# Self-attention's copies before the last rows' high parts, table steps behind the context's row maxima, and the first chunk's weights before the row sums

## The chip, the cores and the metric

The kernel runs on one core of a Trainium2 chip. The metric is the device time of one execution in microseconds (us), lower is better. The same program was timed several times, and each kernel also ran once under the hardware profiler.

## The reference

One decoder layer in float32 on x (16 sequences of 112 rows, 1024 wide) and a context (16 x 375 rows, 1024 wide):

```python
qkv = x @ Wqkv + bqkv                       # q, k, v: 256 wide, one head
x = layernorm(x + softmax(q @ k.T / 16) @ v @ Wo + bo)
Q = x @ Wq.T + bq;  K = ctx @ Wk.T + bk
x = layernorm(x + softmax(Q @ K.T / 32) @ ctx)
Wg, Wu, Wd = dequant(4-bit words, scales, zeros, g_idx)   # FFN, 2752 wide
x = layernorm(x + (silu(x @ Wg) * (x @ Wu)) @ Wd)
```

Matrix products are made in float16 with every operand split into a high and a low part, in three passes (high x high, high x low, low x high).

## The kernel before

Five engine programs are written out by hand, each in its own order, and meet through semaphores. PE is the tensor engine, DVE the vector engine, ACT the scalar engine, POOL is GpSimd, and SP issues most DMAs.

**Self-attention** goes over four groups of four sequences (448 rows). Group 0 stands alone, groups 1 and 2 are one loop on PE, ACT and SP, and group 3 stands alone. In a group PE makes four products for q and k (called f = 0 to 3, 24 matmuls each, into two PSUM banks in turn), the v rows of sequence 0, the scores, the v rows of sequences 1 to 3 (`v_rows`, 24 matmuls each), transposes of the probabilities (L1690), the first half of the transposes of the next group's rows (L1640), the products of probabilities and v, the second half of those transposes, and the output product of each sequence. ACT copies each q/k product out of PSUM (L1371); product f may start when copy f - 2 is made. On DVE a group begins with the largest of the next group's rows (`x_max`, L497), which POOL takes over the partitions, and the low part of the last rows of the group before. Then come the scores' maxima (L543), four steps on the next group's factor (`x_factor`, L512 to L515, which wait for POOL), the reciprocal of the exponentials' sums (L550), the probabilities (L552), two copies of v out of PSUM (L556) and the copy of the transposed probabilities (L561). Then DVE splits the next group's rows (L490) and normalises the four sequences' sums one after the other.

Each normalised sequence is also stored in two float16 parts. ACT makes the high part (`x1_hi`, L1365), which needs the normalised rows and a buffer that an earlier store has to leave. `x1_hi` of sequences 0 to 2 stands at the end of a group's ACT program, and that of sequence 3 behind the copy of f = 0 of the next group.

**Table steps.** The FFN's scales, zeros and indices are made into tables once. `table_rows` runs on DVE in group 1, `table_parts` in group 2 and `select` in group 3, each ahead of the wait for the scores. They are 80-odd short DVE instructions, each waiting for the one before. SP stores their results and reads parts of them back.

**Preparation of cross-attention.** PE multiplies the two weight matrices in float32 (M, eight pieces of 32 matmuls, L1647), POOL takes sums over the same weights (L1213 to L1223), and ACT asks for the next piece of weights (L1415) once PE and POOL have read the last. DVE takes the largest of the first context's rows (L779 and L784), then waits for PE's row of maxima (L789), which stands behind the sixth piece.

**FFN.** 22 chunks of 128 hidden columns. Chunks 0 to 3 multiply gate and up for four groups of 448 rows (t = 0 to 3). The weights of chunk i + 1 (numbers q = 3i + 2 and 3i + 3) and the down weights of chunk i (number 3i + 4) are unpacked meanwhile: PE gathers scales and zeros (L1825, L1899), DVE masks the words (L830, L837) and scales them (L850, L852), ACT and POOL make the parts (L1456, L1245). A gather waits until the weights before it are scaled, because they share PSUM. In the same four chunks the rows' sums for later chunks are made for two sequences each: POOL `row_sums` (L1310 to L1315), ACT `sum_hi` (L1555), DVE `sum_lo` (L1022). `hidden` is silu on ACT, the product with up on DVE, and its parts (L864, L875).

## Time and profile before

| | |
|---|---|
| median of 3 runs | 1846.81 us (1845.61 to 1848.7) |
| the profiled execution: its time, its span | 1848.76 us, 1847.0 us |
| PE busy | 1737.1 us, 94% of the span |
| DVE, ACT, POOL busy | 1069.9 (58%), 494.4 (27%), 502.6 us (27%) |
| mean granted clock of PE | 0.99 of full speed |

The page gives busy time per engine, the span in 40 slices with the granted clock, and the chain of work that ended last. In time order the stages are self-attention (to about 239 us), preparation (to about 367), cross-attention (to about 701), the FFN's products (to about 1445) and the down product. In the last two PE hardly ever waits.

### The profile page before, as it was taken

The numbers are of one execution on the slowest core, as the hardware profiler recorded it, in microseconds if no ns is written. First come the engines' busy times: TensorE is split into PE (matmuls) and PEld (weight loads), VectorE is DVE, ScalarE is ACT, GpSimd is POOL, SyncE is SP. The second block draws the span as 40 slices with busy tenths as digits, with TensorE's granted clock in tenths as the row PEclk, the third lists the DMA queues.
The fourth block names the chain that finished last, engine by engine and source line by source line (L and its number), as shares of the span: only waits on it lengthen the run. The fifth ranks groups of instructions, "written<-read, shape, count | busy, mean of one in ns | idle before, by whom it ended". The sixth has DMA issues, their size and how long they took to land.

```text
span 1847.0 us, 26676 instructions
## 1 busy us (share of the span) xinstructions
PE 1737.1 (94%) x9784; PEld 979.2 (53%) x9784; DVE 1069.9 (58%) x1656; ACT 494.4 (27%) x734; POOL 502.6 (27%) x326
## 2 busy tenths in 40 slices
PE   5898899897899988998999999999999899999998
PEld 3666644486777754444444444444445344444443
DVE  7788550656788875667777777787775211111111
ACT  3222210354555543233323323233232100000000
POOL 0221378223333425543323223223231000000000
PEclk9999999999999999999999999999999999999999
DMA  9342571599999977763231321322313822122120
GB/s 324 102 130 80 158 205 34 120 209 231 225 236 239 232 166 156 179 143 80 56 88 48 81 62 48 95 48 62 81 45 79 324 101 107 53 106 106 53 106 23
DMA packets 335590, 231.89 MB, mean 126 GB/s; under 512 B 288224, under 2 KB 302624, under 8 KB 333348
## 3 DMA queue, kind: packets, MB, share of 16 engines
q1 hardware_dynamic: 329284, 227.85, 47.8%
q10 hardware_dynamic: 6240, 3.15, 0.6%
q8 instruction: 43, 0.70, 0.2%
q14 instruction: 23, 0.19, 0.0%
HBM read 122.93 MB, written 60.83 MB: 99 GB/s over the span
## 4 chain that ended last, share of the span: by engine, by line
PE 45%; issue 28%; DVE 11%; SPq 6%; DMA 5%; POOL 3%; ACT 1%; DVEq 0%; POOLq 0%; ACTq 0%
PE psum L1647 44%; SPq L2178 4%; DMA arena<-arena 3%; DMA arena<-in_x 2%; DVE arena L810 1%; POOL small L1162 1%; POOL arena L1171 1%; PE psum L1899 1%; PE psum L1825 1%; DVE arena L1016 1%; DVE arena L1014 1%; DVE arena L1011 1%; DVE arena L875 1%; DMA x_parts_scratch<-arena 1%; SPq L2085 1%
## 5 line engine op out<-in xcount | busy, mean ns | idle before, releaser
L1647 PE MATMUL psum<-arena 128*128 128x448 f16 (+6 forms) x7176 | 1273.0, 338 | 50.7 <-DMA arena<-arena 24.6
L1647 PEld LDWEIGHTS psum<-arena 128*128 128x128 f16 (+3 forms) x7176 | 752.3, 109 | 552.8 <-issue 89.4
L2002 PE MATMUL psum<-arena 128*128 128x512 f16 x1820 | 393.5, 379 | 6.4 <-DMA arena<-down_weights_scratch 3.7
L2002 PEld LDWEIGHTS psum<-arena 128*128 128x128 f16 x1820 | 177.7, 98 | 222.2 <-DMA arena<-down_weights_scratch 5.4
L1245 POOL TENSOR_TENSOR arena<-arena 128x1024 f16<-128x1024 f32 (+1 forms) x60 | 149.8, 2509 | 417.0 <-ACT arena L1456 417.0
L1144 DVE SCALAR_TENSOR_TENSOR arena<-psum,small,arena 128x512 f32<-128x512 f32 x28 | 20.9, 751 | 331.9 <-PE psum L2002 331.9
L1162 POOL TENSOR_TENSOR small<-small 112x1 f32<-112x1 f32 (+1 forms) x46 | 50.9, 1107 | 510.7 <-DVE small L471 510.7
L1547 ACT ACTIVATE arena<-arena,small 128x448 f32<-128x448 f32 x68 | 45.5, 668 | 208.6 <-DVE arena L1076 145.2
L1456 ACT ACTIVATE arena<-arena 128x1024 f16<-128x1024 f32 (+1 forms) x60 | 68.8, 1173 | 120.2 <-DVE arena L852 91.9
L1236 POOL TENSOR_TENSOR arena<-arena 128x224 f16<-128x224 f32 x64 | 55.6, 869 | 124.9 <-ACT arena L1427 124.8
L850 DVE TENSOR_TENSOR arena<-arena,psum 128x1024 f32<-128x1024 uint32 x65 | 79.1, 1217 | 2.9 <-PE psum L1825 0.9
L852 DVE TENSOR_TENSOR arena<-arena,psum 128x1024 f32<-128x1024 f32 x65 | 79.3, 1221 | 2.2
L1475 ACT ACTIVATE arena<-arena 128x448 f16<-128x448 f32 (+1 forms) x88 | 50.7, 576 | 103.7 <-DVE arena L864 103.7
L875 DVE TENSOR_TENSOR arena<-arena 128x448 f16<-128x448 f32 (+1 forms) x88 | 56.8, 646 | 36.8 <-ACT arena L1475 36.8
L779 DVE TENSOR_REDUCE small<-arena 128x1 f32<-128x1024 f32 (+1 forms) x48 | 58.0, 1216 | 26.5 <-DMA arena<-in_ctx 26.1
L810 DVE SCALAR_TENSOR_TENSOR arena<-arena,small 128x1024 f16<-128x1024 f32 (+1 forms) x48 | 61.2, 1279 | 12.0 <-ACT arena L1433 12.0
L1433 ACT ACTIVATE arena<-arena,small 128x1024 f16<-128x1024 f32 (+1 forms) x48 | 51.8, 1138 | 46.3 <-DVE small L806 46.3
L466 DVE BATCH_NORM_STATS2 small<-arena 112x6 f32<-112x512 f32 (+1 forms) x92 | 58.8, 681 | 1.4 <-DVE small L806 1.1
L482 DVE TENSOR_SCALAR arena<-arena,small 112x1024 f32<-112x1024 f32 (+1 forms) x46 | 44.3, 964 | 25.1 <-POOL small L1162 25.1
L864 DVE SCALAR_TENSOR_TENSOR arena<-arena,small 128x448 f32<-128x448 f32 (+1 forms) x72 | 49.0, 680 | 13.4 <-ACT arena L1484 10.6
L830 DVE TENSOR_TENSOR arena<-arena,small 128x1024 uint32<-128x1024 uint32 x43 | 55.8, 1297 | 0.3
L1252 POOL TENSOR_TENSOR arena<-arena 128x1024 f16<-128x1024 f32 x21 | 44.8, 2132 | 40.0 <-ACT arena L1464 40.0
(213 smaller groups left out, 1207.3 us busy)
## 6 DMA issues: line engine op xcount, KB each, us to landing
h_scratch<-arena SPq DMA_DIRECT2D x84, 224.0 KB, 2.9
arena<-h_scratch SPq DMA_DIRECT2D x13, 1376.0 KB, 6.0
arena<-in_ctx SPq DMA_DIRECT2D x32, 512.0 KB, 5.2
arena<-in_x SPq DMA_DIRECT2D x32, 448.0 KB, 5.6
x_scratch<-arena SPq DMA_DIRECT2D x32, 448.0 KB, 3.6
arena<-x_scratch SPq DMA_DIRECT2D x32, 448.0 KB, 4.7
arena<-in_L_ffn_down_qweight SPq DMA_DIRECT2D x21, 512.0 KB
down_weights_scratch<-arena SPq DMA_DIRECT2D x20, 512.0 KB, 3.8
```

Of the source, the lines that this page charges most:

```text
L466: dve.bn_stats(st[0:n, 6 * h:6 * h + 6], y[:, h * HALF:(h + 1) * HALF]).then_inc(s_st, 1)
L779: ins = dve.tensor_reduce(cmx[0:CP[c], c:c + 1], cx[0:CP[c], c, :], AX.X, ALU.max, apply_absolute_value=True)
L810: dve.scalar_tensor_tensor(cxp[b % 2][0:CP[c], c, 1, :], cx[0:CP[c], c, :], fc[0:CP[c], b:b + 1], cxp[b % 2][0:CP[c], c, 0, :], ALU.mult, ...
L850: dve.tensor_tensor(w, w.bitcast(U32), zeros, ALU.subtract).then_inc(s_dq, 1)
L852: dve.tensor_tensor(w, w, scales, ALU.mult).then_inc(s_wf if done is None else done, 1)
L875: dve.tensor_tensor(h_st[0:n, 1, cols], h_f[0:n, :], h_st[0:n, 0, cols], ALU.subtract).then_inc(s_hl, 1)
L1162: pool.tensor_tensor(rstd[0:n, :], ve[0:n, :], mhalf[0:n, :], ALU.pow).then_inc(s_rstd, 1)
L1245: return pool.tensor_tensor(dst[:, :, 1, :], wf32[:, lo * HALF:hi * HALF].rearrange("p (c n) -> p c n", n=P), dst[:, :, 0, :], ALU.subtract)
L1456: return act.activation(wgu[s][:, lo * 4:hi * 4, 0, :], wf32[:, lo * HALF:hi * HALF].rearrange("p (c n) -> p c n", n=P), ACT.Identity)
L1647: mm = pe.matmul(out, a, r, start=(k == 0), stop=(k == len(pairs) - 1))
L2002: mm = pe.matmul(bk[2 * s + c], ht[s][:, i, a, :], weights_of(i, w, c), start=(i == 0 and (w, a) == PASSES[0]), stop=(i == NI - 1 and (w, ...
L2178: sp.dma_start_transpose(cxt[s].rearrange("p l k t -> p (l k) t")[:, :, c * P:(c + 1) * P], cxp[s][:, c, :, :].rearrange("p l d -> p (l d) ...
```

## The change

1. **Self-attention, ACT.** In the loop groups `x1_hi` of sequence 2 goes from the end of a group to behind the copy of f = 0 of the next group, and that of sequence 3 from behind f = 0 to behind f = 1.
2. **Self-attention, PE and DVE.** `v_rows(3)` goes behind the transposes of the probabilities. DVE does the first v copy, then `x_factor`, then the copy of the transposed probabilities, then the second v copy.
3. **Table steps.** The second part of `table_rows` (now `row_numbers`), `table_parts` and `select` leave groups 1, 2 and 3 and stand between the largest of the first context's rows and the wait for PE's row of maxima. SP's twelve stores of tables go behind the loads of the first context. One memset goes behind the steps, since its place overlaps what they read.
4. **Chunk 0.** DVE scales the up weights of chunk 1 before `hidden(0, 1)` and the first pair's sums, and scales the down weights before the second pair's sums. ACT does `hidden` before `sum_hi` to match.

```diff
@@ dve, self_attention
                 dve.tensor_scalar(nm1[0:S, :], mx1[0:S, :], HD ** -0.5, None, ALU.mult).then_inc(s_nm, 1)
-                if more:
-                    x_factor(g + 1)
                 dve.wait_ge(s_exp, GB * g + GB)
...
+                    if p == 0 and more:
+                        x_factor(g + 1)
+                    if p == 0:
+                        dve.wait_ge(s_pt, g + 1)
+                        dve.tensor_copy(pt[0:S, :, :], bk[4][0:S, 0:TG].rearrange("p (b k) -> p b k", b=GB)
+                                        ).then_inc(s_pte, 1)
...
-            self_attention(2, True, (table_parts,))
-            self_attention(NG - 1, False, (select,))
+            self_attention(2, True)
+            self_attention(NG - 1, False)
...
             for c in range(CC):
                 context_max(0, c)
+            row_numbers()
+            table_parts()
+            select()
+
+            dve.memset(cxp[1][96:P, CC - 1, :, :], 0.0)
             context_largest(0)
@@ dve, chunk
+                if known(i, 1):
+
+                    scaled(q + 1, 1)
+                    hidden(i, 1)
                 for p in pair(i, 0):
                     sum_lo(p)
...
                     masked(down_no(i), 2, s, i)
+                if known(i, 1):
+                    hidden(i, 2)
+                    scaled(down_no(i), 2)
                 for p in pair(i, 1):
                     sum_lo(p)
@@ act, self_attention
-                    if f == 0 and not known(g, 1):
-                        x1_hi(g * GB - 1, GB - 1, 2 * g)
+                    if f < 2 and not known(g, 1):
+                        x1_hi(g * GB - 2 + f, GB - 2 + f, 2 * g)
...
-                for b in range(GB - 1):
+                for b in range(GB - 2 if more else GB - 1):
                     x1_hi(g * GB + b, b, 2 * g + b // 2 + 1)
@@ pe, self_attention
-                for b in range(1, GB):
-                    mm = v_rows(b)
-                    if b % 2:
-                        mm.then_inc(s_v, 1)
+                v_rows(1).then_inc(s_v, 1)
+                v_rows(2)
...
                 mm.then_inc(s_pt, 1)
+                v_rows(3).then_inc(s_v, 1)
```

ACT, from the last `x1_hi` of the loop group to the copies of group 3 (group 3's side shows what stands there in a row). Before:

```order
L1365 ACTIVATE arena<-arena 112x1024
L1404 REGISTER_ALU
L1404 COMPARE_AND_BRANCH
L1371 ACTIVATE arena<-psum,small 128x448
L1365 ACTIVATE arena<-arena 112x1024
L1371 ACTIVATE arena<-psum,small 128x448 x3
```

And now (lines have moved in the changed kernel: L1389 is the copy, L1383 `x1_hi`):

```order
L1383 ACTIVATE arena<-arena 112x1024 x2
L1422 REGISTER_ALU
L1422 COMPARE_AND_BRANCH
L1389 ACTIVATE arena<-psum,small 128x448
L1383 ACTIVATE arena<-arena 112x1024
L1389 ACTIVATE arena<-psum,small 128x448
L1383 ACTIVATE arena<-arena 112x1024
L1389 ACTIVATE arena<-psum,small 128x448 x2
```

Two high parts now stand between the copies, each one copy later, and two instead of three at the group's end.

DVE in chunk 0, from the unpacking of chunk 1's gate weights to the sums of the second pair (L830 and L837 mask, L850 and L852 scale, L1022 is `sum_lo`, L864 and L875 are `hidden`). Before:

```order
L850 TENSOR_TENSOR arena<-arena,psum 128x4x2x128
L852 TENSOR_TENSOR arena<-arena,psum 128x4x2x128
L830 TENSOR_TENSOR arena<-arena,small 128x1024
L1022 SCALAR_TENSOR_TENSOR arena<-arena 112x1024 x2
L864 SCALAR_TENSOR_TENSOR arena<-psum,small,arena 128x448
L875 TENSOR_TENSOR arena<-arena 128x448
L850 TENSOR_TENSOR arena<-arena,psum 128x4x2x128
L852 TENSOR_TENSOR arena<-arena,psum 128x4x2x128
L837 TENSOR_SCALAR arena<-arena,small 128x1024
L1022 SCALAR_TENSOR_TENSOR arena<-arena 112x1024 x2
```

And now (L834, L841, L854, L856, L1030, L868 and L879 are the same lines):

```order
L834 TENSOR_TENSOR arena<-arena,small 128x1024
L854 TENSOR_TENSOR arena<-arena,psum 128x4x2x128
L856 TENSOR_TENSOR arena<-arena,psum 128x4x2x128
L868 SCALAR_TENSOR_TENSOR arena<-psum,small,arena 128x448
L879 TENSOR_TENSOR arena<-arena 128x448
L1030 SCALAR_TENSOR_TENSOR arena<-arena 112x1024 x2
L841 TENSOR_SCALAR arena<-arena,small 128x1024
L868 SCALAR_TENSOR_TENSOR arena<-psum,small,arena 128x448
L879 TENSOR_TENSOR arena<-arena 128x448
L854 TENSOR_TENSOR arena<-arena,psum 128x1024
L856 TENSOR_TENSOR arena<-arena,psum 128x1024
L1030 SCALAR_TENSOR_TENSOR arena<-arena 112x1024 x2
```

The up weights of chunk 1 are scaled two `sum_lo` and one `hidden` earlier.

DVE between the context's row maxima and PE's row of maxima. Before, L789 stood directly behind L784:

```order
L956 MEMSET small 128x4
L957 MEMSET small 128x1
L779 TENSOR_REDUCE small<-arena 128x1 x2
L779 TENSOR_REDUCE small<-arena 119x1
L784 TENSOR_REDUCE small<-small 128x1
L789 TENSOR_REDUCE small<-psum 128x1
```

Now 77 table steps begin behind L788 (the L784 of before); these are the last of them, the memset and what was L789:

```order
L676 MEMSET arena 128x256 x2
L677 MEMSET arena 128x512
L685 TENSOR_SCALAR arena<-arena,small 128x128 x4
L687 TENSOR_SCALAR arena<-arena,small 128x2752
L688 TENSOR_SCALAR arena<-arena,small 128x64
L967 MEMSET arena 32x1024
L793 TENSOR_REDUCE small<-psum 128x1
```

29 of the steps left group 1, 42 left group 2 and six left group 3.

## Rows read from the trace of the kernel before

**Rows 1.** Waits of PE over the whole span: us in total, times, longest.

```profile
PE psum L1647 <- DMA arena<-arena: 24.6, 14, 2.9
PE psum L1647 <- ACT arena L1371: 11.2, 5, 4.6
PE psum L1690 <- DVE arena L556: 5.1, 2, 3.0
PE psum L1647 <- DMA arena<-in_L_xattn_Wq: 0.8, 1, 0.8
```

**Rows 2.** Timeline of PE: start, length, engine, line, form, count, idle before and releaser.

```profile
39.98 21.30 PE L1647 MATMUL psum<-arena 128*128 128x448 f16 x160 [0.33 <-ACT arena L1371]
63.37 0.57 PE L1690 MATMUL psum<-ident,arena 112*112 112x112 f32 x4 [2.09 <-DVE arena L556]
...
93.90 22.76 PE L1647 MATMUL psum<-arena 128*128 128x448 f16 x160 [4.09 <-ACT arena L1371]
...
147.59 22.99 PE L1647 MATMUL psum<-arena 128*128 128x448 f16 x160 [4.64 <-ACT arena L1371]
173.57 0.60 PE L1690 MATMUL psum<-ident,arena 112*112 112x112 f32 x4 [3.00 <-DVE arena L556]
...
201.06 4.71 PE L1647 MATMUL psum<-arena 128*128 128x448 f16 x24 [0.98 <-ACT arena L1371]
206.93 16.76 PE L1647 MATMUL psum<-arena 128*128 128x448 f16 x136 [1.16 <-ACT arena L1371]
...
267.42 55.20 PE L1647 MATMUL psum<-arena 128*128 128x512 f32 x128 [0.83 <-DMA arena<-in_L_xattn_Wq]
...
721.82 1.04 PE L1899 MATMUL psum<-arena 64*128 64x512 bf16 x4 [5.79 <-DVE arena L852]
722.79 19.37 PE L1647 MATMUL psum<-arena 128*128 128x448 f16 x96
...
761.66 18.33 PE L1647 MATMUL psum<-arena 128*128 128x448 f16 x96
```

**Rows 3.** Windows: busy time and count by engine, granted PE clock, DMA share, GB/s.

```profile
93.90:96.00 2.10, 2.10 (x6) 0.87 (x7) 1.91 (x4) 0.00 (x0) 2.10 (x2) 0.50 0.90 250
...
360.00:362.00 2.00, 2.00 (x12) 1.40 (x12) 1.98 (x2) 1.95 (x2) 0.00 (x0) 0.50 2.05 199
...
721.82:724.00 2.18, 2.18 (x8) 0.68 (x9) 0.52 (x1) 0.94 (x1) 2.18 (x2) 0.50 1.24 272
```

**Rows 4.** Timeline of ACT in groups 0 and 1.

```profile
57.72 0.21 ACT L1381 ACTIVATION_READ_ACCUMULATOR arena<-psum,small 112x1 f32 x1
...
92.17 1.06 ACT L1365 ACTIVATE arena<-arena 112x1024 f16<-112x1024 f32 x1 [4.95 <-DMA x_parts_scratch<-arena]
```

**Rows 5.** Timeline of DVE in groups 0, 1 and 2.

```profile
61.72 0.18 DVE L550 RECIPROCAL small<-small 112x4 f32<-112x4 f32 x1
...
105.67 0.15 DVE L618 TENSOR_SCALAR small<-small 128x1 int32<-128x1 int32 x1
...
110.81 0.62 DVE L543 TENSOR_REDUCE small<-psum 112x4 f32<-112x448 f32 x1
...
157.06 0.16 DVE L643 TENSOR_SCALAR small<-small 128x3 f32<-128x3 f32 x1
...
169.34 0.62 DVE L543 TENSOR_REDUCE small<-psum 112x4 f32<-112x448 f32 x1
```

**Rows 6.** Timeline of DVE in the preparation.

```profile
322.88 0.29 DVE L789 TENSOR_REDUCE small<-psum 128x1 f32<-128x128 f32 x1 [57.57 <-PE psum L1744]
```

**Rows 7.** Timeline of POOL in the preparation and in chunk 0.

```profile
254.28 2.96 POOL L1213 TENSOR_TENSOR arena<-arena,small 128x1024 f32<-128x1024 f32 x1 [0.26 <-POOL small L1207]
...
264.79 1.90 POOL L1213 TENSOR_TENSOR arena<-arena,small 128x1024 f32<-128x1024 f32 x1 [0.18 <-POOL arena L1223]
...
728.59 2.13 POOL L1245 TENSOR_TENSOR arena<-arena 128x1024 f16<-128x1024 f32 x1
```

**Rows 8.** Line L1415, ACT's six loads of weight pieces: time to landing.

```profile
DMA to landing us min/median/max: 3.9/4.0/9.9
```

More of the change, by code:

```diff
@@ L559, in self_attention @@
                                              ALU.add).then_inc(s_ve, 1)
-                dve.wait_ge(s_pt, g + 1)
-                dve.tensor_copy(pt[0:S, :, :], bk[4][0:S, 0:TG].rearrange("p (b k) -> p b k", b=GB)).then_inc(s_pte, 1)
+                    if p == 0 and more:
[4 more added lines that the diff above has]
+                                        ).then_inc(s_pte, 1)
                 if more:
@@ L612, in table_rows, with row_numbers @@
                 T["idx"] = steps[0]
+            def row_numbers():
                 dve.wait_ge(s_const, 4)
@@ L952, in _ @@
             x1_lo(NB - 1, GB - 1)
-            for i in range(2):
-                dve.memset(cxp[i][96:P, CC - 1, :, :], 0.0)
+            dve.memset(cxp[0][96:P, CC - 1, :, :], 0.0)
             factor_step(dve.memset(cmx, 0.0))
@@ L1031, in chunk @@
                     masked(q + 1, 1, 1 - s, e + s)
+                if known(i, 1):
+                    scaled(q + 1, 1)
+                    hidden(i, 1)
                 for p in pair(i, 0):
                     sum_lo(p)
-                hidden(i, 1)
+                if not known(i, 1):
+                    hidden(i, 1)
+                    if more:
+                        scaled(q + 1, 1, s_cmb if mixed(i + 1) else None)
                 if more:
-                    scaled(q + 1, 1, s_cmb if mixed(i + 1) else None)
                     masked(down_no(i), 2, s, i)
+                if known(i, 1):
+                    hidden(i, 2)
+                    scaled(down_no(i), 2)
                 for p in pair(i, 1):
@@ L1042, in chunk @@
                     weight_sums(q + 1, i + 1)
-                hidden(i, 2)
-                if not is_last(i):
+                if not known(i, 1):
+                    hidden(i, 2)
+                if not known(i, 1) and not is_last(i):
                     scaled(down_no(i), 2)
@@ L1568, in chunk @@
                     high_part(q, 1 - s, 0)
+                if known(i, 1):
+                    hidden(i, 1)
                 for p in pair(i, 0):
                     sum_hi(p)
-                hidden(i, 1)
+                if not known(i, 1):
+                    hidden(i, 1)
                 if more and not mixed(i + 1):
                     high_part(q + 1, 1 - s, 1)
+                if known(i, 1):
+                    hidden(i, 2)
                 for p in pair(i, 1):
@@ L1577, in chunk @@
                     high_sums(q + 1, 1 - s)
-                hidden(i, 2)
+                if not known(i, 1):
+                    hidden(i, 2)
                 if not is_last(i):
@@ L2166, in _ @@
             store_parts(NB - 1, (NB - 1) % 2)
+            sp.wait_ge(s_t, T["parts"])
+            for k in range(3):
+                for m in range(2):
+                    sp.dma_start(tabr_d[m, k * GU:(k + 1) * GU, :].rearrange("g n -> (g n)").rearrange("(p c) -> p c", p=P),
+                                 parts[:, k, at_fl[m]:at_fl[m + 1]]).then_inc(s_tabo, 16)
+                sp.dma_start(dtab_d[k * GD:(k + 1) * GD, :].rearrange("g n -> (g n)").rearrange("(p c) -> p c", p=P),
+                             parts[:, k, at_fl[2]:]).then_inc(s_tabo, 16)
+            for m in range(2):
+                sp.dma_start(tabr_d[m, 3 * GU:, :].rearrange("g n -> (g n)").rearrange("(p c) -> p c", p=64),
+                             z_bf[0][64 * m:64 * m + 64, :]).then_inc(s_tabo, 16)
+            sp.dma_start(dtab_d[3 * GD:, :].rearrange("g n -> (g n)").rearrange("(p c) -> p c", p=P),
+                         z_bf[1]).then_inc(s_tabo, 16)
             sp.wait_ge(s_t, T["sel"])
```

12 lines of the change are left out of this document (removed).

## Prediction

> **What bounds the kernel now.** I read the waits of PE first, then PE's timeline around each, then the timeline of the engine named. PE is busy nearly all the time, so the kernel gets shorter only where a wait of PE goes, or where PE runs at a higher clock. The change speaks to the waits for ACT's copies (five, 11.2 us), the two for DVE's v copy (5.1 us), one for a weight load (0.8 us) [rows 1], and the 5.79 us before the down gather of chunk 0 [rows 2]. The longest total, 24.6 us for DMA transposes [rows 1], lies in cross-attention, where the order stays.
>
> The waits have a second cost. After the wait of 4.09 us the granted clock is 0.50, the lower level of 1.2 GHz instead of 2.4, and so it is after the wait of 5.79 us [rows 3]. The same 160 matmuls took 21.30 us in group 0, after a wait of 0.33, but 22.76 and 22.99 in groups 1 and 2. The 96 matmuls behind the 5.79 us took 19.37 us, and 18.33 one chunk later [rows 2]. I count these differences with the waits.
>
> **Group 0.** DVE held the reciprocal until its factor steps were done, at 61.72, though ACT had finished the exponentials at 57.93 [rows 4, 5]. PE's transposes began 1.65 us after the reciprocal began, at 63.37 [rows 2]. With the factor behind the first v copy the reciprocal can start at 58.0, so the transposes could at 59.7. PE gets there at 58.6: it was done with all v rows at 63.37 - 2.09 = 61.28, and v_rows(3), now behind the transposes, is 2.7 us. That 2.7 is taken from the 21.30 us piece: a v product is 24 matmuls of 256 columns, and by columns 96 of those plus 48 of 448 and the short scores share it that way. A wait of 1.1 remains of 2.09. Gain **1.0** (bounds 0 and 2.1).
>
> **Group 1.** ACT began its high part of sequence 2 at 92.17, after 4.95 us for a store, and the copy of f = 0 was behind it [rows 4]. PE started f = 2 at 93.90, and could have at 89.81 [rows 2]. Now the copy of f = 0 stands ahead of that high part, so the 4.09 us go, and 22.76 - 21.30 = 1.46 us of low clock with them. The copy of f = 1 is now behind the high part. It ends near 93.23 + 0.7 = 93.9, and f = 3 is due at 89.8 + 4.6 = 94.4 (f = 2 is 24 matmuls, a quarter of the 18.33 us [rows 2]), so half a microsecond is to spare.
> What comes late next is DVE. It made the maxima at 110.81, and 5.14 us of table steps stood right before, from 105.67 [rows 5]. These leave, so the maxima start at 105.7. From maxima to PE's transposes took 173.57 - 169.34 = 4.23 us in group 2, where DVE was the last [rows 2, 5]. That gives 109.9. PE reaches the transposes at 89.8 + 21.3 - 2.7 = 108.4 and waits 1.5. Gain 4.09 + 1.46 - 1.5 = **4.0** (bounds 2 and 5.5).
>
> **Group 2.** The same for its 4.64 us and 22.99 - 21.30 = 1.69 us. The wait of 3.00 us for the v copy [rows 2] goes too if DVE is early enough. 12.28 us of steps leave, so the maxima start at 157.06 instead of 169.34 [rows 5], and the transposes could start at 161.3. PE reaches them at 147.59 - 4.64 + 18.6 = 161.55. Gain **9.3** (bounds 6 and 9.3). The second v copy, now after v_rows(3), is covered by the next rows' transposes on PE in groups 0 to 2.
>
> **Group 3** loses its waits of 0.98 and 1.16 us [rows 2]. There are no next rows, so the second v copy stands bare behind v_rows(3), but a wait for the copy of the probabilities stood there before. Gain **2.1** (bounds 0 and 2.5). What is left of self-attention, DVE's splitting, normalising and the loads it waits for, hangs on PE's output products and moves as a whole.
>
> **Preparation.** 77 table steps come to DVE here, about 20 us. DVE sat idle 57.57 us before L789, until 322.88 [rows 6], so I cost them at nothing. If they took longer than 57 us, DVE would be late for the context's parts. SP's twelve table stores move behind the first context's loads. SP next waits for DVE's steps, and behind it stand only the selection store, the read-back of tables, two residual loads and the second context's loads. The last wait for the parts that DVE makes after L789, so nothing due is blocked. PE waited 0.83 us for a weight piece [rows 2] whose load took 9.9 us against a median of 4.0 [rows 8], among the context's loads and the selection's store. The store and the read-back leave that moment. I take **0.8** (bounds -2, if the twelve stores hit another piece, and 0.8).
>
> **Chunk 0.** The down gather waited 5.79 us for the up weights' scaling, which stood behind two sums' low parts and a hidden part. Now the scaling follows the gathers at once, and nothing else that the gather needs is late by the code. So 5.79 goes, with 19.37 - 18.33 = 1.04 of low clock and about 0.4 on the gather itself (1.04 us long at the low clock). The next thing late is POOL. Its low part of the up weights still stands behind the second pair's row sums and ends at 728.59 + 2.13 = 730.7 [rows 7]. PE needs it after three quarters of the 96 matmuls, at 716.0 + 0.6 + 13.8 = 730.4, and waits 0.3. Gain **6.9** (bounds 3 and 7.3).
>
> The sum is 1.0 + 4.0 + 9.3 + 2.1 + 0.8 + 6.9 = 24.1 us. The profiled execution took 1848.76 us, so it would take 1824.7. The median of the runs shown is 1.95 us below the profiled time, so I predict **1822.7 us**, 1.3% less.
>
> **The port that DVE and POOL share.** POOL's first product took 2.96 us while DVE ended its group, and 1.90 us ten microseconds later [rows 7]. So table steps on DVE can stretch POOL's sums, and POOL's product of a piece must be done before ACT asks for the weights of the piece after next. By the Trainium skill (SBUF — State Buffer, section on the two separate sides) an instruction of either engine that takes the shared pair of ports holds it to its end and the other fully blocks. The row agrees in direction, and the rule speaks against this move. Priced by rows: if POOL stood still for the whole 20 us, the load of one piece would come 20 us late. A piece takes PE 55.20 / 4 = 13.8 us and a load 4.0 us [rows 2, 8], so 9.8 us of it is covered and PE would wait 10.6. The time would be 1833.3. Against it: most of the 77 steps are on one or a few columns. Chance 0.04.
>
> **Rivals.**
> - *The wait moves to f = 3.* The copy of f = 1 has half a microsecond to spare behind a high part that waits for a store. If the stores land some us later, PE waits there, and long enough for the clock to fall. At worst that returns the two waits, about 8 us: 1830.7. For it: the small margin. Against it: the store is issued where it was. Chance 0.12.
> - *Chunk 0 waits for POOL.* If row sums and low part stretch beside DVE's earlier scaling, PE waits for the low part instead and only some 2 us are won: 1827.6. Chance 0.06.
> - *The gain is lost in cross-attention.* It has 24.6 us of waits for transposes [rows 1]. If they were set by something that does not move with the stage, the first 17.2 us would come back there: 1839.9, or 1846.8 if chunk 0 fails as well. Against it: those loads are issued after this stage's own work. Chance 0.04, half of it at no change.
> - *Slower: the low clock stays.* Between 360 and 362 us PE was busy all 2.00 us and still had 0.50 [rows 3], among short waits. The new order leaves waits of 1 to 1.5 us before the transposes in groups 0 and 1. If these kept the clock low, each 1 us of full-clock work would cost 1 us more. The change is a loss from 24.1 us of such work on. Groups 1 and 2 have some 47 us each (147.59 - 93.90, less the waits and the low clock's share [rows 2]), so low through both gives 1822.7 + 94 = 1917. Against it: the waits of 2.09 and 3.00 us in this trace were followed by pieces of normal length. Chance 0.04.
>
> **How the numbers follow.** The forecast has 0.70, the rivals 0.12, 0.06, 0.04 and 0.04, the shared port 0.04. The time is the forecast's. With every bound at its good end the sum is 27.5, which gives 1819.3. The range reaches a little below, to 1819, and up to 1831 for the first two rivals, with the rest above it. Every case but the last and half of the cross-attention one is faster by more than 0.2% (3.7 us, about what a measurement of this kernel can tell from no change): faster 0.94, same 0.02, slower 0.04.
>
> **What would show it.** No wait for L1371's copy above 1 us in groups 1 to 3, no granted clock of 0.50 there, and 160 matmuls in about 22 us with the wait for the v copy among them. In group 1 a wait of about 1.5 us before the transposes. DVE busy with the steps soon after the context's maxima, and still idle for 30 us or more before PE's row. The down gather of chunk 0 without a wait. PE's M stage about 16.5 us earlier and chunk 1 about 24 us earlier. I am wrong if PE waits for f = 3, if POOL's sums hold up a weight piece, or if cross-attention takes longer than its 334 us.

## The result, and the profile after

The changed kernel takes **1820.63 us** (median of six runs, 1816.36 to 1822.58) against 1846.88 us (six runs of the kernel before, 1844.94 to 1850.56): ratio 0.9853, 95% interval 0.9837 to 0.9868. The forecast was 1822.7 us with a range of 1819 to 1831. The profiled execution took 1816.36 us (span 1814.6 us), the fastest of the six and 4.3 us under their median. So a second profile of the same kernel was taken later (e10_again, span 1821.1 us, 1822.87 us), and the sizes below are read from both.

Waits of PE over the whole span of the changed kernel (us in total, times, longest):

```profile
PE psum L1671 <- DMA arena<-arena: 21.9, 14, 2.8
...
PE psum L1671 <- DVE arena L820: 5.1, 2, 3.3
...
PE psum L1922 <- DVE arena L1024: 3.9, 1, 3.9
...
PE psum L1671 <- ACT arena L1389: 0.3, 1, 0.3
```

The five waits for ACT's copies [rows 1], 11.2 us, are one of 0.3 us. The total for DMA transposes in cross-attention, where the order stayed, is 21.9 us here and 24.4 in the second profile, against 24.6 before. PE's timeline in self-attention and at chunk 0's down gather, first profile:

```profile
60.30 0.57 PE L1712 MATMUL psum<-ident,arena 112*112 112x112 f32 x4 [0.75 <-DVE arena L554]
...
77.48 30.39 PE L1671 MATMUL psum<-arena 128*112 128x512 f16 x196 [0.90 <-DVE arena L586]
107.70 0.55 PE L1712 MATMUL psum<-ident,arena 112*112 112x112 f32 x4
...
124.89 30.39 PE L1671 MATMUL psum<-arena 128*112 128x512 f16 x196 [0.93 <-DVE arena L586]
155.12 0.55 PE L1712 MATMUL psum<-ident,arena 112*112 112x112 f32 x4
...
172.31 30.39 PE L1671 MATMUL psum<-arena 128*112 128x512 f16 x196 [0.93 <-DVE arena L586]
202.54 0.55 PE L1712 MATMUL psum<-ident,arena 112*112 112x112 f32 x4
...
691.59 0.61 PE L1922 MATMUL psum<-arena 64*128 64x512 bf16 x4 [0.42 <-DMA arena<-down_selection_scratch]
692.13 18.33 PE L1671 MATMUL psum<-arena 128*128 128x448 f16 x96
```

From the last output products of one group to the transposes of the next PE runs 30.39 us in one piece, three times alike. The granted clock behind the old waits is back at the full level (columns: window, its length, busy time and count of PE, PEld, DVE, ACT, POOL, granted clock, DMA share, GB/s):

```profile
92.00:94.00 2.00, 2.00 (x13) 1.06 (x11) 1.81 (x4) 0.00 (x0) 2.00 (x2) 1.00 0.93 248
```

Before, the window from 93.90 had 0.50 [rows 3]. The down gather of chunk 0 waits 0.42 instead of 5.79 us, and the 96 matmuls behind it take 18.33 instead of 19.37 us [rows 2]. The second profile of the same kernel, at group 1's transposes:

```profile
78.03 30.49 PE L1671 MATMUL psum<-arena 128*112 128x512 f16 x196 [0.89 <-DVE arena L586]
110.14 0.59 PE L1712 MATMUL psum<-ident,arena 112*112 112x112 f32 x4 [1.62 <-DVE arena L554]
```

Here is the wait of 1.5 us that the prediction asked for and the first profile lacks. It stands in four of the five profiles in which self-attention is as the change makes it (1.60 to 1.62 us).

**Where the time went**, in us won on PE against the profile before, stage by stage. Groups 1 and 2 run from the start of one group's transposes of the next rows to the next group's. Group 0 begins with PE's f = 2 and group 3 ends with its first output product.

| step | predicted | first profile | second profile |
|---|---|---|---|
| start-up (unchanged) | 0 | -0.9 | -1.7 |
| group 0 | 1.0 | 1.3 | 1.6 |
| group 1 | 4.0 | 5.7 | 3.8 |
| group 2 | 9.3 | 9.7 | 9.7 |
| group 3 | 2.1 | 2.6 | 2.6 |
| preparation | 0.8 | 0.8 | 0.3 |
| cross-attention (unchanged) | 0 | 5.6 | 1.9 |
| chunk 0 | 6.9 | 6.8 | 7.3 |
| the rest (unchanged) | 0 | 0.7 | 0.4 |
| sum (spans) | 24.1 | 32.4 | 25.9 |

Each column compares single executions, and these differ where nothing was changed. In e4 (below), whose self-attention is that of the kernel before, groups 0 to 3 took 184.9 us instead of the 188.6 of the profile before. Against these two the change's two profiles (169.2 and 170.9 us) won 13.9 to 19.3 us there. The forecast for the four groups was 16.4.

**The surprise is on DVE in the preparation.** First profile, the 77 steps in their new place, and PE's row of maxima behind them (L793):

```profile
247.34 0.14 DVE L622 TENSOR_SCALAR small<-small 128x1 int32<-128x1 int32 x1
...
263.18 5.72 DVE L665 TENSOR_SCALAR arena<-arena,small 128x172 f32<-128x172 f32 x3
...
277.74 7.38 DVE L672 TENSOR_SCALAR arena<-arena 128x43 uint32<-128x43 uint32 x8
...
302.35 2.21 DVE L688 TENSOR_SCALAR arena<-arena,small 128x64 bf16<-128x64 bf16 x1
304.83 0.91 DVE L967 MEMSET arena<- 32x1024 uint32 x1 [0.27 <-DVE arena L688]
305.75 0.29 DVE L793 TENSOR_REDUCE small<-psum 128x1 f32<-128x128 f32 x1
...
319.43 3.67 DVE L814 SCALAR_TENSOR_TENSOR arena<-arena,small 128x1024 f16<-128x1024 f32 x3 [7.23 <-ACT arena L1451]
```

They run from 247.34 to 304.56 us, 57.2 us where they had taken some 20 in the groups, and fill the 57.57 us of idle time [rows 6] to the end. DVE does not wait for PE's row any more. PE's row was ready before DVE came for it:

```profile
303.10 0.38 PE L1767 MATMUL psum<-ident,small 128*128 128x128 f32 x2
```

It ended at 303.48 us and DVE read it at 305.75, 2.3 us later (1.3 us later in the second profile). What is left of DVE's cover is the 7.23 us before L814 (8.22 in the second profile).

### The profile page after: what moved, and what is told of

It is laid out like the page before. It is cut to its first block, busy times and chain, and to the rows that moved or that the text cites. A ratio compares the mean times of both kernels' runs of the same rounds, so it can differ in the third digit from the quotient of the medians.

```text
span 1814.6 us, 26677 instructions
## 1 busy us (share of the span) xinstructions
PE 1729.8 (95%) x9784; PEld 976.8 (54%) x9784; DVE 1106.1 (61%) x1656; ACT 494.1 (27%) x734; POOL 500.2 (28%) x326
## 4 chain that ended last, share of the span: by engine, by line
PE 53%; issue 25%; DVE 10%; SPq 5%; DMA 4%; ACT 1%; POOL 1%; DVEq 0%; POOLq 0%; ACTq 0%
PE psum L1671 51%; SPq L2201 4%; DMA arena<-arena 3%; DVE arena L814 1%; DVE arena L490 1%; PE psum L1922 1%; PE psum L1848 1%; DVE arena L1024 1%; DVE arena L1022 1%; DVE arena L1019 1%; PE psum L1684 1%; DVE arena L879 1%; DMA arena<-in_L_attn_Wqkv 1%; DVE arena L997 1%; POOL small L1180 1%
## 5 line engine op out<-in xcount | busy, mean ns | idle before, releaser
L1671 PE MATMUL psum<-arena 128*128 128x448 f16 (+6 forms) x7176 | 1266.9, 337 | 34.5 <-DMA arena<-arena 21.9
L1162 DVE SCALAR_TENSOR_TENSOR arena<-psum,small,arena 128x512 f32<-128x512 f32 x28 | 20.9, 751 | 331.5 <-PE psum L2025 331.5
L854 DVE TENSOR_TENSOR arena<-arena,psum 128x1024 f32<-128x1024 uint32 x65 | 79.1, 1218 | 3.0 <-PE psum L1848 0.9
L856 DVE TENSOR_TENSOR arena<-arena,psum 128x1024 f32<-128x1024 f32 x65 | 79.3, 1221 | 2.2
L879 DVE TENSOR_TENSOR arena<-arena 128x448 f16<-128x448 f32 (+1 forms) x88 | 58.2, 661 | 36.8 <-ACT arena L1493 36.8
L783 DVE TENSOR_REDUCE small<-arena 128x1 f32<-128x1024 f32 (+1 forms) x48 | 57.8, 1215 | 24.6 <-DMA arena<-in_ctx 24.2
L814 DVE SCALAR_TENSOR_TENSOR arena<-arena,small 128x1024 f16<-128x1024 f32 (+1 forms) x48 | 61.2, 1279 | 9.8 <-ACT arena L1451 9.7
L868 DVE SCALAR_TENSOR_TENSOR arena<-arena,small 128x448 f32<-128x448 f32 (+1 forms) x72 | 49.0, 680 | 13.4 <-ACT arena L1502 10.6
L834 DVE TENSOR_TENSOR arena<-arena,small 128x1024 uint32<-128x1024 uint32 x43 | 55.8, 1299 | 0.3
L482 DVE TENSOR_SCALAR arena<-arena,small 112x1024 f32<-112x1024 f32 (+1 forms) x46 | 40.2, 873 | 24.6 <-POOL small L1180 24.6
L1270 POOL TENSOR_TENSOR arena<-arena 128x1024 f16<-128x1024 f32 x21 | 45.7, 2176 | 33.3 <-ACT arena L1482 33.3
```

The lines of the kernel that those rows point to most:

```text
L783: ins = dve.tensor_reduce(cmx[0:CP[c], c:c + 1], cx[0:CP[c], c, :], AX.X, ALU.max, apply_absolute_value=True)
L814: dve.scalar_tensor_tensor(cxp[b % 2][0:CP[c], c, 1, :], cx[0:CP[c], c, :], fc[0:CP[c], b:b + 1], cxp[b % 2][0:CP[c], c, 0, :], ALU.mult, ...
L854: dve.tensor_tensor(w, w.bitcast(U32), zeros, ALU.subtract).then_inc(s_dq, 1)
L856: dve.tensor_tensor(w, w, scales, ALU.mult).then_inc(s_wf if done is None else done, 1)
L879: dve.tensor_tensor(h_st[0:n, 1, cols], h_f[0:n, :], h_st[0:n, 0, cols], ALU.subtract).then_inc(s_hl, 1)
L1671: mm = pe.matmul(out, a, r, start=(k == 0), stop=(k == len(pairs) - 1))
```

## The experiments

There were twelve runs: eleven kernels, and e10_again, which is the changed kernel once more. e8_pool_less leaves a term of the scores out, so it is a probe and no candidate. "Prep. end" is where PE starts the 240 matmuls behind the preparation; cross-attention runs from there to the first gate gather of chunk 1, and chunk 0, as counted here, from that gather to the next chunk's. These three columns come from one profiled execution each, in us.

| kernel | median us (range) | ratio, 95% | prep. end | cross-att. | chunk 0 |
|---|---|---|---|---|---|
| before | 1846.88 | | 367.8 | 333.7 | 40.6 |
| the change | 1820.63 | 0.984 to 0.987 | 348.5 | 328.1 | 33.8 |
| e1_act_only | 1849.16 (1838.8 to 1852.0) | 0.9975 to 1.001 | 364.6 | 336.1 | 41.7 |
| e2_order_only | 1852.85 (1851.4 to 1858.4) | 1.0014 to 1.0043 | 372.6 | 332.7 | 40.8 |
| e3_tables_only | 1841.65 (1836.5 to 1846.5) | 0.9946 to 0.998 | 361.0 | 335.0 | 41.7 |
| e4_chunk0_only | 1840.88 (1834.5 to 1850.5) | 0.9952 to 0.999 | 365.4 | 329.1 | 33.5 |
| e5_no_tables | 1849.44 (1843.6 to 1855.1) | 0.9988 to 1.0026 | 375.9 | 334.3 | 33.3 |
| e6_numbers_back | 1828.70 (1826.3 to 1831.3) | 0.9865 to 0.9916 | 356.2 | 334.3 | 33.3 |
| e7_numbers_4x | 1829.72 (1826.9 to 1835.1) | 0.9873 to 0.9927 | 358.9 | 332.1 | 33.6 |
| e8_pool_less | 1820.75 (1819.3 to 1829.7) | 0.9826 to 0.9884 | 350.4 | 331.5 | 33.6 |
| e9_turn | 1824.09 (1821.9 to 1828.4) | 0.9841 to 0.9882 | 350.9 | 334.8 | 33.3 |
| e10_again | 1822.87 (1819.9 to 1825.9) | 0.9832 to 0.9874 | 351.6 | 331.7 | 33.3 |
| e11_no_order | 1821.74 (1820.6 to 1824.5) | 0.983 to 0.987 | 351.1 | 331.1 | 33.3 |
| e12_no_act | 1833.88 (1830.5 to 1839.3) | 0.9892 to 0.9935 | 365.9 | 331.3 | 33.4 |

Ratios are to the kernel before as measured beside each run; its medians were 1847.47 (e1 to e4), 1846.36 (e5 to e8) and 1848.45 (e9 to e12).

### One part alone

**e1_act_only**, ACT's part on the kernel before:

```diff
-                    if f == 0 and not known(g, 1):
-                        x1_hi(g * GB - 1, GB - 1, 2 * g)
+                    if f < 2 and not known(g, 1):
+                        x1_hi(g * GB - 2 + f, GB - 2 + f, 2 * g)
...
-                for b in range(GB - 1):
+                for b in range(GB - 2 if more else GB - 1):
```

> Of the whole change only ACT's part: the high parts of two sequences go one copy later. Theory A (the copies and DVE's table steps are two chains that end at nearly the same time, so PE gains only the smaller of the two): the 4.09 and 4.64 us for the copies of f = 0 go, but the table steps still stand before DVE's maxima (about 110.8 and 169.3 us), so the transposes of the probabilities now wait for DVE in groups 1 and 2. Gain in group 1 about 2 us, in group 2 none, in group 3 about 2: 3 to 5 us in all, time 1842 to 1844, and a new wait of 2 to 5 us per group before the transposes. Theory B (the parts add up, each wait is worth its own length and its low clock): 4.09 + 1.46 + 4.64 + 1.69 + 2.1 = 14 us, time 1833.

PE's timeline of e1 in groups 1 and 2:

```profile
112.43 0.59 PE L1690 MATMUL psum<-ident,arena 112*112 112x112 f32 x4 [2.03 <-DVE arena L556]
...
129.69 30.48 PE L1647 MATMUL psum<-arena 128*128 128x448 f16 x208
170.16 0.99 PE L1690 MATMUL psum<-ident,arena 112*112 112x112 f32 x4 [10.00 <-DVE arena L556]
```

The waits for the copies are gone, and in group 2 PE stands 10.00 us at the transposes, at the lower clock afterwards (0.99 us for four transposes that take 0.55). By the medians no gain can be measured. The profile bears theory A out up to the preparation's end, which comes 3.2 us earlier: group 1 is 3.5 us shorter, group 2 is 1.0 us longer, and group 3 wins nothing where 2 us were expected. Cross-attention and chunk 0, where nothing was changed, took 3.5 us more in that execution.

**e2_order_only**, the order of v rows, factor and copies (PE's part of the edit; DVE's is as in the change):

```diff
-                for b in range(1, GB):
-                    mm = v_rows(b)
-                    if b % 2:
-                        mm.then_inc(s_v, 1)
+                v_rows(1).then_inc(s_v, 1)
+                v_rows(2)
...
+                v_rows(3).then_inc(s_v, 1)
```

> Only PE's third and fourth v rows behind the transposes and DVE's factor behind the first v copy. Both theories: group 0 gains about 1.0 to 1.4 us (the wait of 2.09 shrinks to about 1). In groups 1 and 2 the copies of ACT still hold PE, and in group 2 the same maxima at about 169.3 us hold the transposes at 173.6 us: PE waits 2.7 us more there, but has the v rows behind it, so about 2 us can be won. Time 1843.5 to 1846.

A miss in sign: 5.4 us **slower**. In group 2:

```profile
172.38 1.00 PE L1690 MATMUL psum<-ident,arena 112*112 112x112 f32 x4 [6.65 <-DVE arena L554]
173.16 4.24 PE L1649 MATMUL psum<-arena 128*112 128x256 f16 x24
177.25 1.94 PE L1642 MATMUL psum<-ident,arena 112*128 112x112 f32 x16
```

While DVE is late, PE waits at the transposes in any case. Before, the 2.8 us of v_rows(3) were done inside that wait. Now they stand behind it, at the lower clock (4.24 us), and the next rows' transposes start at 177.25 us, where they had started at 174.01. Group 1 is 1.7 and group 3 is 1.6 us longer as well. Only group 0 is shorter, by 1.1 us.

**e3_tables_only**, the table steps and their stores moved on the kernel before (DVE's part of the edit):

```diff
-            self_attention(2, True, (table_parts,))
-            self_attention(NG - 1, False, (select,))
+            self_attention(2, True)
+            self_attention(NG - 1, False)
...
+            row_numbers()
+            table_parts()
+            select()
```

> Only the table steps moved. Theory A: in groups 1 and 2 PE is held by ACT's copies, the maxima come 5 and 12 us earlier and wait for PE's scores, so only the 3.00 us before group 2's transposes and the 0.8 us for a weight piece are won: about 4 us, time 1843. Theory B (table steps were the bound in both groups): 5.1 + 12.3 us, time 1829. In the preparation the 77 steps should again take 50 to 58 us on DVE instead of the 20.4 us that they took in the groups, and DVE should reach PE's row of maxima less than 5 us before or after the row is ready.

5.8 us won (4 expected by theory A, 17 by theory B). ACT's copies still hold PE in groups 1 and 2, 4.34 us in group 1 and 2.03 and 1.23 us in group 2. DVE is done with the steps at 317.3 us, and reads PE's row at 318.47 without a wait for it, some 2.3 us after it was ready, as expected.

**e4_chunk0_only**, chunk 0's part on the kernel before (the first of its places):

```diff
+                if known(i, 1):
+
+                    scaled(q + 1, 1)
+                    hidden(i, 1)
                 for p in pair(i, 0):
                     sum_lo(p)
...
```

> Only chunk 0's new order. Theory: the part is independent of the rest and wins 6.8 us (5.79 of wait, 1.04 of low clock): time 1840, down gather's wait below 0.6 us, the 96 matmuls behind it 18.3 us instead of 19.4. Rival: the 6.8 us between the two profiles come in part from the earlier stages (cross-attention's end is different), and alone it wins 3 us or less, with a wait for POOL's low part of the up weights.

6.6 us won by the medians, 1.8 to 8.9 by the interval, with chunk 0 at 33.5 us instead of 40.6 and no wait at the down gather. The part is independent of the rest, as expected: chunk 0 takes 33.3 to 33.8 us in every kernel that has it.

### One part left out

**e5_no_tables**, the change with the table steps in their old places (`row_numbers` is a part of `table_rows` again, and SP's stores are back too):

```diff
-            self_attention(2, True)
-            self_attention(NG - 1, False)
+            self_attention(2, True, (table_parts,))
+            self_attention(NG - 1, False, (select,))
```

> The change without its table part: copies ahead, v rows behind the transposes, chunk 0's order, and the table steps where they were. Theory A (the moves meet at the transposes of the probabilities): PE comes to them at about 155 us in group 2, DVE's maxima still stand behind the steps at about 163 to 166 us, so PE waits 10 to 14 us, and self-attention wins 0 to 3 us of its 18.5. With chunk 0's 6.8 us the time is 1837 to 1841. Theory B (parts add up): only the 6 us that the table part won alone are missing, 1826 to 1827.

The whole gain is gone: 27 to 29 us above the changed kernel's two medians. Chunk 0 still takes 33.3 us, so its 7 us are won there and lost again in self-attention. PE in groups 1 and 2, and DVE in group 2:

```profile
114.90 0.99 PE L1706 MATMUL psum<-ident,arena 112*112 112x112 f32 x4 [6.74 <-DVE arena L554]
115.69 4.10 PE L1665 MATMUL psum<-arena 128*112 128x256 f16 x24
...
176.50 0.99 PE L1706 MATMUL psum<-ident,arena 112*112 112x112 f32 x4 [11.85 <-DVE arena L554]
177.29 4.02 PE L1665 MATMUL psum<-arena 128*112 128x256 f16 x24
```

```profile
162.53 1.00 DVE L663 TENSOR_SCALAR arena<-arena,small 128x172 f32<-128x172 f32 x3
...
166.46 1.88 DVE L670 TENSOR_SCALAR arena<-arena 128x43 uint32<-128x43 uint32 x8
...
172.24 0.62 DVE L543 TENSOR_REDUCE small<-psum 112x4 f32<-112x448 f32 x1
```

The clock behind the wait of 11.85 us (columns as above):

```profile
177.00:179.00 2.00, 2.00 (x11) 1.99 (x10) 0.71 (x2) 0.00 (x0) 0.00 (x0) 0.50 0.01 4
```

Theory A had the waits right (10 to 14 us in group 2) but the total too good: the stages up to the preparation's end became 8 us longer instead of 0 to 3 shorter. It left out what e2 shows, v_rows(3) on DVE's path.

**e6_numbers_back**:

```diff
-            self_attention(1, True, (table_rows,))
+            self_attention(1, True, (table_rows, row_numbers))
...
-            row_numbers()
             table_parts()
```

> The changed kernel with the 29 row-number steps (5.1 us) back in group 1. If DVE's maxima bind PE in group 1 with nothing to spare (in the changed kernel they stand at 103.6 us and PE comes to the transposes at 107.7 without a wait), they stand at 108.7, the v copy ends near 112.6, and PE waits about 4.9 us, with a low clock of 1 to 1.5 us behind it: 1825 to 1827. If DVE had several us in hand there, the time stays at 1820.6. In the preparation the steps end about 9 us earlier (295 instead of 304.8 us), which wins nothing.

A cost of 5.8 to 8.1 us, by the two medians of the changed kernel, for 5.1 us of steps, and more than the 4 to 6 expected. DVE's maxima stand at 110.05 us, PE waits 6.78 us, and v_rows(3) follows at the lower clock (3.96 us). The expectation started from the first profile, in which PE did not wait here. From the 1.62 us of the second profile, 5.1 us more give the 6.78 measured. DVE has nothing to spare in group 1. The 240 matmuls behind the preparation took 26.26 instead of 24.69 us, with a granted clock of 0.57 from 356 to 360 us. They took 26.36 us in e12 as well. Whether this is an effect of the edits is not shown.

**e11_no_order**, the change with e2's part undone (PE's part of the edit):

```diff
-                v_rows(1).then_inc(s_v, 1)
-                v_rows(2)
+                for b in range(1, GB):
+                    mm = v_rows(b)
+                    if b % 2:
+                        mm.then_inc(s_v, 1)
...
-                v_rows(3).then_inc(s_v, 1)
```

> The change without its order part (v rows before the transposes, factor before the reciprocal). With the table steps gone DVE is early: in group 1 the v copy would end near 108.2 us and PE comes to the transposes at 110.4. So only group 0's 1.0 us and up to 1 us in group 3 come back: 1821.5 to 1823. Rival: the order part is what lets PE through in groups 1 and 2, and 2.7 us come back in each: 1826 or more.

**e12_no_act**, the change with e1's part undone:

```diff
-                    if f < 2 and not known(g, 1):
-                        x1_hi(g * GB - 2 + f, GB - 2 + f, 2 * g)
+                    if f == 0 and not known(g, 1):
+                        x1_hi(g * GB - 1, GB - 1, 2 * g)
```

> The change without ACT's part. The waits of 4.1 and 4.6 us for the copy of f = 0 and of about 1 and 1.2 us in group 3 return, with 1.5 and 1.7 us of low clock behind the long ones: 12 to 14 us, 1832 to 1835. That part alone had won nothing (1849.2 against 1847.5), so if each part has a worth of its own, the time stays near 1820.6.

Without the order part nothing measurable is lost. Without ACT's part 11 to 13 us are lost, and the five waits for ACT's copies are back with 12.1 us. So the worths differ by what else is there: ACT's part 0 alone and 12 in the change; the order part -5 alone and 0 in the change; the table part 6 alone and 27 to 29 in the change.

### The cover in the preparation

**e7_numbers_4x**:

```diff
-            row_numbers()
+            for _ in range(4):
+                row_numbers()
             table_parts()
```

> The changed kernel with the 29 row-number steps made four times in the preparation (same values each time). One pass took 9.3 us there beside GpSimd's sums, so three more take 24 to 28 us. Theory 1 (the 57.5 us of idle time were used up by the move, and only the later idle of 7.2 us is left before PE waits for DVE): DVE reaches PE's row of maxima at 328 to 333 instead of 305.7 us, and the time grows by 12 to 22 us, to 1833 to 1843. Theory 2 (the prediction's: 20 us of steps under 57 us, 30 or more are left): no change, 1820.6.

PE's and DVE's timeline of e7:

```profile
339.72 0.77 PE L1768 MATMUL psum<-ident,small 128*128 128x128 f32 x2 [7.31 <-DVE small L788]
```

```profile
321.82 0.29 DVE L793 TENSOR_REDUCE small<-psum 128x1 f32<-128x128 f32 x1
...
328.31 3.68 DVE L814 SCALAR_TENSOR_TENSOR arena<-arena,small 128x1024 f16<-128x1024 f32 x3
339.41 0.16 DVE L788 TENSOR_REDUCE small<-small 128x1 f32<-128x4 f32 x1
```

DVE reads PE's row 14 us later than in the second profile (308.13) and 17 us after it was ready, the idle time before L814 is used up, and PE waits 7.31 us for the second context's maxima. The time grows by 7 to 9 us. That is less than the 12 to 22 us of theory 1, but it refutes theory 2, by which 30 us or more were left. The added passes cost DVE less than 24 us, since some of the steps now met GpSimd's idle stretches (L672 at 306.07 us: 1.89 us for eight, against 7.38).

**e8_pool_less**:

```diff
-                pool.tensor_tensor(part, wk[:, bass.ds(m, 1), :].rearrange("p o d -> p (o d)"),
-                                   bqc[:, bass.ds(m, 1)].to_broadcast([P, D]), ALU.mult).then_inc(s_pu, 1)
-                pool.wait_ge(s_pu, 2 * m + 1)
-                pool.tensor_tensor(acc_v, acc_v, part, ALU.add).then_inc(s_pu, 1)
+                pool.sem_inc(s_pu, 2)
```

> GpSimd leaves out the product and sum of the second weight vector (acc_v, two of its six instructions per piece, 4.3 of 9.5 us), so that term of the scores is missing. Theory 1 (an instruction of GpSimd keeps DVE's two-operand or several-column steps out until it ends, so these 77 steps go at about one per GpSimd instruction): with GpSimd idle for more than half of the stretch the steps take 25 to 38 us instead of 57.5, single ones of 0.15 to 0.9 us. Theory 2 (the steps are slower here because of something else: PE's float32 weight loads, DMA, the buffers' place): still 50 us or more. The whole time stays within 3 us of 1820.6 by both, since PE bounds the stage.

```profile
249.26 0.14 DVE L622 TENSOR_SCALAR small<-small 128x1 int32<-128x1 int32 x1
...
262.25 0.99 DVE L665 TENSOR_SCALAR arena<-arena,small 128x172 f32<-128x172 f32 x3
...
277.80 0.24 DVE L688 TENSOR_SCALAR arena<-arena,small 128x64 bf16<-128x64 bf16 x1
...
305.60 0.29 DVE L793 TENSOR_REDUCE small<-psum 128x1 f32<-128x128 f32 x1 [26.38 <-PE psum L1764]
```

The steps take 28.8 us instead of 57.2, DVE is idle for 26.38 us before L793, and the kernel takes the same time (1820.75 us). That is theory 1. The changed kernel's own rows show how it works. DVE, first profile:

```profile
251.32 0.15 DVE L632 TENSOR_SCALAR small<-small 128x1 int32<-128x1 int32 x1
...
253.45 2.20 DVE L640 TENSOR_SCALAR small<-small 128x2 int32<-128x2 int32 x1
...
256.69 1.36 DVE L647 TENSOR_SCALAR small<-small 128x3 f32<-128x3 f32 x1
...
261.20 1.76 DVE L660 TENSOR_TENSOR small<-small 128x1 f32<-128x1 f32 x1
```

and POOL:

```profile
251.30 1.89 POOL L1238 TENSOR_TENSOR arena<-arena,small 128x1024 f32 x1 [0.21 <-POOL arena L1236]
253.27 2.36 POOL L1241 TENSOR_TENSOR arena<-arena 128x1024 f32<-128x1024 f32 x1
256.13 1.90 POOL L1231 TENSOR_TENSOR arena<-arena,small 128x1024 f32<-128x1024 f32 x1 [0.50 <-POOL arena L1241]
...
261.05 1.89 POOL L1238 TENSOR_TENSOR arena<-arena,small 128x1024 f32 x1 [0.21 <-POOL arena L1236]
```

Of DVE's steps here, three began inside a GpSimd instruction and end with it: 253.45 + 2.20 = 255.65 beside 253.27 + 2.36 = 255.63, 256.69 + 1.36 = 258.05 beside 258.03, 261.20 + 1.76 = 262.96 beside 262.94. The step at 251.32, on one column with one tensor operand, ran its 0.15 us beside L1238 unhindered. In the first profile some 30 of the 77 steps are held like this.

### A version meant to beat both

**e9_turn**, chunk 3's pair sums earlier, on DVE, ACT and GpSimd alike (DVE's part):

```diff
+                turn = i == NP - 1
+                if turn:
+                    sum_lo(2 * i)
                 if not known(i, 1):
                     hidden(i, 0)
...
+                if turn:
+                    sum_lo(2 * i + 1)
```

> A version meant to beat the changed kernel. In chunk 3 the sums of the first pair (ACT's high, DVE's low part) go ahead of hidden(3, 0), the second pair's row sums on GpSimd go ahead of the gate weights' low part, their parts ahead of hidden(3, 1), and the weight sums ahead of the masked down words. If GpSimd's row sums of the last pair are what is late behind the 3.93 us before chunk 3's down gather (they began at 797.6 us in the changed kernel, 13.6 us after the pair before), the weight sums end near 805 instead of 809 us, that wait falls below 1 us and the low clock behind it goes: 4 to 5.4 us, 1815 to 1817. Rival: hidden(3, 0) or hidden(3, 1) comes late instead and PE waits there: no gain.

Beside it ran **e10_again**, the changed kernel as it is:

> The changed kernel once more, beside the others of this job, and with another profile. If the 5.6 us by which cross-attention was shorter in its first profile are spread between executions (the same stage took 328.1 to 336.1 us in the profiles so far, with nothing changed in it), this profile can have any of these lengths, and the median is 1820.6 within 2 us. If the change shortened the stage, it is again near 328 us.

A miss for e9: 1824.09 us against 1822.87 of the changed kernel beside it, no gain, and the wait before chunk 3's down gather grew from 3.93 to 5.98 us. POOL in e9:

```profile
802.93 1.28 POOL L1335 TENSOR_TENSOR arena<-arena 112x512 f32<-112x512 f32 x1 [9.47 <-DMA arena<-x_scratch]
```

GpSimd was free for the last pair 9.47 us before its rows came. SP loads them behind the chunk's weights and tables, and that place had not been moved. An SP order with this load ahead was not tried.

The median is 2.2 us above the first, just outside the 2 us expected. The second profile has cross-attention at 331.7 us. Over all 14 profiles the stage lies between 328.1 and 336.1 us, and it took 329.1 in e4, whose earlier stages are unchanged. So nothing shows that the 5.6 us of the first profile are a part of the change's worth; the spread between executions is enough for them.

## Why the prediction was right, and where a step was not

**Total.** Forecast 24.1 us; the medians say 26.2 and, beside e10, 25.6. The stages that the change touches give 27.0 us in the first profile and 25.3 in the second.

**Group 0**: 1.0 predicted, 1.3 and 1.6 measured. The wait left is 0.52 to 0.95 us instead of 1.1. That the order part won this is not shown. From f = 2 to the next rows' transposes group 0 took 21.6 to 23.8 us in the five profiles with the old order, and 22.2 to 22.7 in the nine with the new. The profile before is the longest of the five, and e4's, without any wait at this place, the shortest. So it is partly luck that this term came out right.

**Group 1**: right, by its own steps. The maxima stood at 103.6 us in the first profile and at 105.3 to 106.2 in four others (predicted 105.7), with the predicted wait of 1.5 us at 1.60 to 1.62. The first profile's 1.7 us more come from which engine was first at a shared port, told in the last section.

**Group 2**: 9.3 predicted, 9.7 in both. The prediction put ACT's copies and DVE's table steps into one sum and let the later of the two decide. e1 (10.00 us of new wait), e3 (7.6 us of waits for copies stay in groups 1 and 2) and e5 show that this is how they stand to each other.

**Group 3**: 2.1 predicted, 2.6 in both.

**Preparation**: the 0.8 us are right in the mean at best. The wait for the weight piece is there in all five profiles with the steps in their old places (0.8 to 1.3 us), and in two of nine with them moved (0.84 and 0.32).

**The step that failed** is "77 table steps come to DVE here, about 20 us", and with it "still idle for 30 us or more before PE's row". They took 57.2 us. That they still cost nothing was luck: the cover had just this length, and another 7 us stood behind it. e7 shows that more would have cost. The **shared-port rival** had the collision right and the victim wrong. It let GpSimd stand for DVE's 20 us. In fact GpSimd issued sums almost without a gap, mostly of 0.45 to 2.4 us each, and kept 1.90 us for L1231 as before [rows 7]. Its sums over the eight pieces took 70.6 to 70.7 us in all, against 69.8 before, so it lost about 1 us, while the steps that were held got in at the gaps between its sums. What the prediction put against the rival, that most steps are on one or a few columns, did not protect DVE: steps on two or three columns were held. The Trainium skill (SBUF — State Buffer, section on the two separate sides) says that the shared pair is "an exclusive lock, not a bandwidth split" and that whichever starts first gets it for the whole instruction. By that rule, read from DVE's side, a waiting step ends just after the instruction that it met. The trace agrees: the three steps of the changed kernel shown in e8's section ended 0.02 us after it. The measurements do not agree everywhere with the rule on who gets the port: in the profile of e8 a row of DVE that began 0.07 us ahead of GpSimd's instruction was held (last section). As a price for PE (10.6 us, 1833.3) the rival did not occur.

**Chunk 0**: 6.9 predicted, 6.8 and 7.3 measured; no wait for POOL's low part.

**Other rivals.** PE did not wait for f = 3 in the two profiles of the change, but less was to spare than the half microsecond forecast: in e5, e9 and e11 it waited 0.27 to 0.30 us for that copy. The gain was not lost in cross-attention. The low clock did not stay after the waits of 0.5 to 1.6 us. It did follow the waits of 6.65 to 11.85 us in e1, e2, e5 and e6, and v_rows(3) then cost 4.0 to 4.2 instead of 2.8 us (in e1 it stands ahead of the wait). In e4 a wait of 3.79 us was followed by a granted clock of 0.50 too, for more than 5 us.

## What to carry to other kernels

Moves on two chains that end at the same instruction have no worth of their own: here the parts were worth 0, -5, 6 and 7 us alone by the medians, 8 in sum, and 26 together, so price them in one sum per stage and test them by leaving one out, not only one in. Moving work behind a point where an engine waits is free only if it no longer waits there; while it waits, the moved work lands on the path. Steps moved into an engine's idle time must be priced by what the neighbour on its port does there, not by what they took where they stood.

## What the runs showed of the hardware

DVE's 77 steps took 2.8 times as long beside GpSimd's sums (57.2 us against the 5.1 + 12.3 + 3.0 of the three groups), while GpSimd lost about 1 us. Of the steps that began inside a GpSimd instruction, those of the forms TENSOR_TENSOR (two tensor operands, one column too), TENSOR_SCALAR on two or more columns and CAST on 512 columns were all held, and those on one to three columns ended within 0.03 us of the GpSimd instruction. TENSOR_SCALAR and CAST on one column, RECIPROCAL on three columns (0.18 us inside L1236) and MEMSET on 1 to 512 columns passed. It was so in e10's and e3's profiles too.

The same port makes executions differ. In group 0 DVE's row L482 (a normalised sequence) and GpSimd's product (L1189) start within 0.3 us of each other. First profile of the change, DVE, then POOL:

```profile
83.32 0.81 DVE L482 TENSOR_SCALAR arena<-arena,small 112x1024 f32<-112x1024 f32 x1 [0.45 <-POOL small L1180]
```

```profile
83.62 2.74 POOL L1189 TENSOR_TENSOR arena<-arena 112x1024 f32<-112x1024 f32 x1 [0.34 <-DMA arena<-in_x]
```

and the second profile, DVE, then POOL:

```profile
83.94 2.83 DVE L482 TENSOR_SCALAR arena<-arena,small 112x1024 f32<-112x1024 f32 x1 [0.45 <-POOL small L1180]
```

```profile
83.88 2.35 POOL L1189 TENSOR_TENSOR arena<-arena 112x1024 f32<-112x1024 f32 x1
```

Where DVE came first it took 0.81 us and GpSimd's 2.35 us became 2.74. Where GpSimd was first, DVE took 2.83 us, its later work in the group stood 2 us later, and PE waited 1.62 us in group 1. In the other three profiles with the change's self-attention (e7, e8, e9) L482 was held as well, for 2.83 to 2.97 us, and PE waited 1.60 or 1.61. Of all 14 profiles 11 have L482 held in group 0, the profile before among them. In that one L482 of group 1 was held too (2.93 us), and in e4 neither was, which fits its shorter self-attention. The recorded starts do not always tell the loser: in e8 L482 began 0.07 us ahead of GpSimd's product and still took 2.97 us.
